# Cross-attention and a 16-expert layer on one core: outputs of the experts computed turned, with gates put on the hidden values, and first products eight experts ahead

## The reference, cut to what matters

```python
# x: (8, 56, 128); ctx: (8, 1500, 128); 16 heads of 64; HIDDEN 256; 14 routed + 2 shared experts
x = x + tanh(g_xattn) * attention(layernorm(x), ctx, ctx)      # causal by index: only keys 0..55 count
xf = layernorm(x).reshape(448, 128)
gates = softmax(xf @ router_w)                                 # (448, 14)
masked = top2(gates); masked = masked / (masked.sum(-1) + 1e-9)
def ffn(rw, W1, W2):
    h = xf * rsqrt(mean(xf * xf) + 1.1920929e-07) * rw
    return silu(h @ W1) @ W2
routed = einsum('end,ne->nd', [ffn(e) for e in routed_experts], masked)
x = x + tanh(g_ffn) * (routed + sum(ffn(s) for s in shared_experts))
```

## Time and profile before

| | |
|---|---|
| runs | 117.8, 117.86, 119.21 us |
| profiled execution | 117.94 us, its span 116.1 us (first to last instruction) |
| PE busy | 107.2 us, 92% |
| DVE, ACT, POOL busy | 69.3, 59.4, 43.8 us |
| clock granted to PE | full in every slice |
| DMA | 13.76 MB, all loads landed by 40.3 us |

### The profile page before, as it was taken

The page is one execution under the profiler, slowest core; times in us unless marked ns, Lnnn a source line. Parts: engine busy times, 40 slices in busy tenths (PEclk is TensorE's granted clock), DMA queues, the critical chain, the costliest instruction groups (busy, mean ns, idle before and its releaser), DMA issues.

```text
span 116.1 us, 2394 instructions
## 1 busy us (share of the span) xinstructions
PE 107.2 (92%) x826; PEld 91.6 (79%) x826; DVE 69.3 (60%) x195; ACT 59.4 (51%) x99; POOL 43.8 (38%) x75
## 2 busy tenths in 40 slices
PE   6699999996999999999699999999999999999980
PEld 6687768745496487488489989999999999999970
DVE  0068966659688789879843329999333333333360
ACT  5053787943579579579964298333333333333300
POOL 7803599000001000100101798666666666663000
PEclk9999999999999999999999999999999999999999
DMA  3899999999997000000000000000000000000003
GB/s 90 254 295 285 416 413 413 420 420 444 421 428 308 28 0 0 0 6 0 0 0 6 0 6 0 3 3 0 0 6 0 0 0 0 0 0 0 0 0 79
DMA packets 3169, 13.76 MB, mean 119 GB/s; under 512 B 431, under 2 KB 1007, under 8 KB 2775
## 3 DMA queue, kind: packets, MB, share of 16 engines
q1 hardware_dynamic: 3159, 13.63, 31.3%
HBM read 13.40 MB, written 0.23 MB: 117 GB/s over the span
## 4 chain that ended last, share of the span: by engine, by line
PE 57%; DVE 14%; DMA 12%; ACT 8%; SPq 4%; issue 3%; DVEq 0%; ACTq 0%
PE score_ps L736 15%; DMA ctx_all<-in_ctx_dram 12%; PE attn_ps L736 8%; PE ring L729 6%; PE ring L731 6%; PE ring L730 6%; PE ring L597 5%; ACT square_junk L816 4%; PE score_ps L552 4%; PE attn_ps L621 3%; DVE probs L1046 3%; DVE row_sum L1039 2%; DVE row_max L1025 2%; DVE probs L1032 2%; PE score_ps L546 2%
## 5 line engine op out<-in xcount | busy, mean ns | idle before, releaser
L938 ACT ACTIVATE mixT<-ring 128x896 f32<-128x896 f32 x16 | 14.6, 917 | 26.9 <-PE ring L731 26.9
L736 PE MATMUL score_ps<-w,mixT 128*112 (+1 forms) x160 | 19.1, 273 | 0.2 <-ACT mixT L938 0.2
L736 PEld LDWEIGHTS score_ps<-w,mixT 128*112 128x112 f32 x160 | 18.7, 177 | 0.8 <-issue 0.3
L437 POOL TENSOR_TENSOR h_scale<-h_base,minus_half 112x1 f32<-112x1 f32 x4 | 2.2, 547 | 41.7 <-DVE h_base L1069 41.7
L1210 DVE SCALAR_TENSOR_TENSOR xn_rows<-score_ps,gates,xn_rows 112x128 f32<-112x128 f32 x36 | 10.1, 343 | 11.5 <-PE score_ps L736 11.3
L621 PEld LDWEIGHTS attn_ps<-wkq_space,mixT 128*112 128x112 f32 x128 | 14.2, 177 | 2.4 <-issue 2.4
L621 PE MATMUL attn_ps<-wkq_space,mixT 128*112 128x128 f32 x128 | 15.0, 276 | 0.0
L402 POOL TENSOR_TENSOR w_full<-w,columns 128x256 f32 (+1 forms) x16 | 9.8, 612 | 11.5 <-PE ring L731 10.5
L729 PE MATMUL ring<-hT_hi,w_hi 128*128 128x448 f32 (+2 forms) x36 | 13.9, 386 | 0.1
L731 PE MATMUL ring<-hT_hi,w_lo 128*128 128x448 f32 (+2 forms) x36 | 12.6, 350 | 0.0
L730 PE MATMUL ring<-hT_lo,w_hi 128*128 128x448 f32 (+2 forms) x36 | 12.6, 349 | 0.0
(11 more groups left out here) (136 smaller groups left out, 186.7 us busy)
## 6 DMA issues: line engine op xcount, KB each, us to landing
ctx_all<-in_ctx_dram SPq DMA_DIRECT2D x4, 1500.0 KB, 18.8
w<-in_w_dram SPq DMA_DIRECT2D x2, 1792.0 KB, 27.3
wkq_space<-in_wkq_dram SPq DMA_DIRECT2D x2, 512.0 KB, 6.1
wvo<-in_wvo_dram SPq DMA_DIRECT2D x1, 1024.0 KB, 10.6
w<-in_w_shared_dram SPq DMA_DIRECT2D x2, 256.0 KB, 16.4
ctx_head<-in_ctx_head_dram SPq DMA_DIRECT2D x1, 480.0 KB, 8.9
ctx_headT<-in_ctx_headT_dram SPq DMA_DIRECT2D x1, 224.0 KB, 4.9
x_space<-in_x_rows_dram SPq DMA_DIRECT2D x1, 224.0 KB, 5.7
```

What stands on the lines that cost most here:

```text
L736: last = nc.tensor.matmul(dst, hidden[slot][:, c, t * ROWS:(t + 1) * ROWS], w2_chunk(c), start=(c == 0), stop=(c == 1))
L938: nc.scalar.activation(hidden[slot], ring[:, 2 * slot:2 * slot + 2, 0:TOKENS], ACT.Silu).then_inc(S["hidden_ready"], 1)
```

## The change

- **Outputs turned.** `w2` is now the weight operand and `hidden` moves, 448 columns at a time; all experts add into one PSUM bank, `out_sums`, with the model dimension on the partitions. Experts 0 to 3 (`WHOLE`) use two fp32 products (L885); experts 4 to 15 (`PARTED`) use six fp32r products (L897, L899, L903). The output is (128, 448), turned back on the host.
- **Gates on hidden.** DVE multiplies the 128x896 hidden values of each routed expert by a tile of gates (L1454); for parted experts ACT rounds (L1121) and DVE subtracts (L1463). The gates of experts 2, 3 and 4 are spread over the partitions by PE (L942); those of 5 to 15 are stored to DRAM and loaded again with a broadcast, in four loads (L453, L456). The shared experts' gate is multiplied into their second weights by POOL (L578). PE also turns `x1` (L930) and the gates (L936).
- **First products ahead.** Eight hidden slots in the space of `keyproj`. PE does the first products of experts 2 to 9 before or between outputs 0 to 3, and is then seven ahead; ACT's order of Silu and rounding follows it. The loops are written out.
- **POOL.** It splits the first weights of all 16 experts and the second weights of 12, mostly while attention runs. `w_hi` is now a cast of `w_full` and waits for it. The four `h_scale` stand between these pieces.
- **SP.** The context keeps two pieces (four batches) at a time; its third and fourth piece wait for squares of earlier batches. Weights go through staging space (`stage_pair`, `ctx_head`, `wvo`), in pieces of four experts, each behind a wait for what used the space before.

```diff
+WHOLE = [0, 1, 2, 3]
+PARTED = [e for e in range(EXPERTS) if e not in WHOLE]
+FULL_SLOTS = 8
+PART_SLOTS = 4
+GATE_GROUPS = [(3, 4), (4, 5), (5, 7), (7, ROUTED)]
...
+            context(0)
+            context(1)
+            sp.dma_start(w2_whole[:, 0:SHARED, :, :], A["w2_shared"]).then_inc(S["w2_shared_loaded"], 16)
...
+            sp.wait_ge(S["ctx_lo_ready"], 1)
+            first_four(0)
+            sp.wait_ge(S["w1_scaled_ready"], SHARED)
...
+            wait_filled(sp, "M3")
+            first_four(1)
+            first_four(2)
+            context(2)
+            sp.wait_ge(S["w1_scaled_ready"], 6)
+            second_four(0)
+            context(3)
...
+            def split_w1(experts):
...
+                    nc.gpsimd.tensor_tensor(w1_full[:, :], first_weights(e),
+                                            rms_cols[:, e:e + 1].to_broadcast([P, HIDDEN]), ALU.mult)\
+                        .then_inc(S["w1_full_ready"], 1)
+                    pool.wait_ge(S["w1_full_ready"], e + 1)
+                    nc.gpsimd.tensor_copy(w1_hi[:, e, :], w1_full[:, :])\
+                        .then_inc(S["w1_hi_ready"], 1)
...
+            def split_w2(experts):
+                for e in experts:
+                    n = PARTED.index(e)
+                    weights = second_weights(e).rearrange("p (c d) -> p c d", c=2)
+                    pool.wait_ge(w2_loaded[n // 4], 16)
+                    nc.gpsimd.tensor_copy(w2_hi[:, n, :, :], weights)\
...
+            split_w1(range(6))
...
+            nc.gpsimd.tensor_copy(spread[:, :, :], ones).then_inc(S["spread_ready"], 1)
+            split_w1(range(6, 12))
+            second_scale(0)
+            split_w1(range(12, EXPERTS))
+            second_scale(1)
+            split_w2(range(4, 8))
...
+            second_scale(2)
+            split_w2(range(8, 12))
+            second_scale(PAIRS - 1)
...
+            def next_hidden(e):
+                pe.wait_ge(S["hidden_ready"], e - 1)
+                hidden_products(e).then_inc(S["hidden_filled"], 1)
...
+            for e in range(6, 9):
+                next_hidden(e)
+            output_whole(2)
+            next_hidden(9)
+            for e in range(3, EXPERTS - 1):
+                if e in WHOLE:
+                    output_whole(e)
+                else:
+                    output_parted(e, out_sums).then_inc(S["expert_done"], 1)
+                if e + AHEAD - 1 < EXPERTS:
+                    next_hidden(e + AHEAD - 1)
...
+            for e in range(9, EXPERTS):
+                round_hidden(e - 4)
+                silu(e)
...
-            def add_expert(place, gate, before=moe):
-                for t in range(PAIRS):
-                    last = nc.vector.scalar_tensor_tensor(
...
+                dve.wait_ge(S["hidden_ready"], e + 1)
+                nc.vector.tensor_tensor(hidden(e), hidden(e), tile.unsqueeze(1)
+                                        .to_broadcast([P, 2, TOKENS]), ALU.mult)\
+                    .then_inc(S["hidden_gated"], 1)
...
+            for e in range(SHARED, EXPERTS):
+                gate_hidden(e)
+                if e - 1 in PARTED:
+                    subtract_hidden(e - 1)
+            subtract_hidden(EXPERTS - 1)
```

More of the change, by code:

```diff
@@ new lines, in output_parted @@
+            def output_parted(e, sums, cols=slice(0, TOKENS)):
+                n = PARTED.index(e)
+                hi, lo = (hidden_part(slots, e) for slots in (hi_slots, lo_slots))
+                pe.wait_ge(S["w2_split_ready"], n + 1)
+                pe.wait_ge(S["hidden_hi_ready"], n + 1)
+                alone = e == EXPERTS - 1
+                for c in range(2):
+                    nc.tensor.matmul(sums, w2_hi[:, n, c, :], hi[:, c, cols],
+                                     start=(alone and c == 0), stop=False)
+                    nc.tensor.matmul(sums, w2_lo[:, n, c, :], hi[:, c, cols],
+                                     start=False, stop=False)
+                pe.wait_ge(S["hidden_lo_ready"], n + 1)
+                for c in range(2):
+                    last = nc.tensor.matmul(sums, w2_hi[:, n, c, :], lo[:, c, cols],
+                                            start=False, stop=(e >= EXPERTS - 2 and c == 1))
+                return last
@@ new lines, in _, with spread_gates @@
+            last.then_inc(S["x1T_filled"], 1)
+            next_hidden(4)
+            pe.wait_ge(S["gates_ready"], 1)
+            for t in range(PAIRS):
+                last = nc.tensor.transpose(gatesT_ps[:, t * ROWS:(t + 1) * ROWS], gates[:, t, :],
+                                           ident[0:ROWS, 0:ROWS])
+            last.then_inc(S["gatesT_filled"], 1)
+            next_hidden(5)
+            def spread_gates(n):
+                nc.tensor.matmul(gate_banks[n], spread[:, n, :], gates_parts, start=True, stop=True)\
+                    .then_inc(S["gate_spread"], 1)
@@ L960, in _ @@
+            for e in range(5, 9):
+                silu(e)
+            round_hidden(4)
+            for e in range(9, EXPERTS):
+                round_hidden(e - 4)
+                silu(e)
+            for e in range(EXPERTS - 4, EXPERTS):
+                round_hidden(e)
         @block.vector
@@ L1205, in wide @@
                 return col[:, :].unsqueeze(2).to_broadcast([ROWS, PAIRS, ROUTED])
-            def add_expert(place, gate, before=moe):
-                for t in range(PAIRS):
-                    last = nc.vector.scalar_tensor_tensor(
-                        out=moe[:, t, :], in0=out_banks[place][0:ROWS, t * D:(t + 1) * D],
-                        scalar=gate(t), in1=before[:, t, :], op0=ALU.mult, op1=ALU.add)
-                last.then_inc(S["acc_done"], 1)
-            def static_gate(e):
-                return lambda t: gates[:, e, t:t + 1]
             dve.wait_ge(S["logits_filled"], 1)
```

392 lines of the change are left out of this document (235 added, 157 removed).

## The result

| | before | changed |
|---|---|---|
| median of the runs side by side | 117.83 us | 120.5 us (119.93 to 121.09) |
| profiled execution: time, span | 117.94, 116.1 us | 120.87, 119.0 us |
| `x1` of tile 3 taken up by DVE (end of attention) | 62.39 us | 70.16 us |
| from there to the end of DVE's last addition | 51.08 us | 46.76 us |
| from there to the end of the span | 2.63 us | 2.08 us |

The changed kernel takes 1.022 of the time before (95% interval 1.015 to 1.030; measured again with more runs: 1.0215, 1.0165 to 1.0264). It is slower, by 2.1 to 2.2%, and neither interval tells whether that is over 2%. Forecast was 118.3 us, 0.4% slower, range 114.0 to 122.2.

A forecast was written before the change was run, and what follows sets the result against it. Before: PE bounds the expert layer, hand-overs attention. After: attention ends at 69.4 us (7.0 late), expert 5 gated from 88.2, DVE done 113.0, closing 1.5, store 2.1: span 116.6, time 118.3 us, range 114.0 to 122.2.

The forecast's parts named there:

- POOL's chain: Attention: POOL's list runs without pause from 25.6 us, h_scale of tile 2 comes 7.4 us late, attention ends 7.0 late.
- The cast: POOL's cast of 256 elements, shown by no row: taken as 0.39 us, between ends of 0.26 and 0.61.
- Collisions: Attention: six two-input DVE normalisations meet a busy POOL and lose 0.15 us each, 0.9 us in all.
- The 1.2 us that this rule was said to add for the casts: Attention: if any GpSimd operation locks the shared ports, casts collide too and the sum is some 1.2 us higher.
- The gates' path: Start of expert layer: DVE's gate operations take 4.6 us, then 6.8 us until expert 5 can be gated, at 88.2.
- the way through DRAM shifts 23 DVE operations one for one: Rival on late gates, expert layer: each delay reaches the end; 2 us more gives 120.3 us; chance 0.07.
- DVE behind the gates: Expert layer from 88.2 us: 11 multiplications and 12 subtractions take 23.0 us, plus 1.7, last subtraction ends at 113.0.
- PE's 5.6 us are given away to POOL's lateness and to DVE: Summary: POOL's lateness (7.0 us) and DVE's two 1 us operations an expert behind the gates use up PE's gain.
- PE's gain itself: Expert layer: turned outputs save PE 7.2 us, transposes and spreading products add about 1.6, 5.6 gained if PE stayed bound.
- The end behind it: Kernel end, behind the closing addition at 114.5 us: a single store issue until the span ends, 2.1 us.
- The clock: Rival: PE idles near 48 and 61 us, half clock adds 3.8 us on the last attention output: 122.1; chance 0.10.
- the rival on collisions: Attention and gates: normalisations lose up to 0.6 us each, up to 3 us more, 119.5 to 121.5 us; chance 0.18.

The follow-up runs named there:

- e_scales_first: Changed kernel with POOL's list reordered, h_scale of tiles 0, 1, 2 behind 9, 13, 15 first weights, second weights behind the third scale: 114.06 us, ratio 0.963.
- b_late: Kernel before with 14, 4, 3 and 2 triples of scratch work on POOL ahead of the four scales, making them late: 127.63 us, ratio 1.076.
- e_warm: Changed kernel with 60 bf16 products on zeros, meant for PE's wait near 48 us: 121.98 us, ratio 1.029.
- b_busy: Kernel before with 8, 4, 4 and 3 triples of scratch work on POOL ahead of the four scales, none late: 118.74 us, ratio 1.008.
- b_casts: b_busy with the added POOL work made of one-input casts and copies alone (11, 6, 6, 4 triples): ratio 1.009.
- s_gates_late: e_scales_first with the gates stored to DRAM twice before they are loaded, about 1.7 to 2 us later: 115.08 us, ratio 0.974.
- e_dve_less: Changed kernel with DVE's subtractions of experts 8 to 15 over 56 of 448 tokens only, 6.3 us less DVE work: 119.7 us, ratio 1.014.
- s_pe_less: e_scales_first without the product of the second weights' low part in the twelve parted experts, 4.9 us less for PE: 113.0 us, ratio 0.960.
- s_early_product: e_scales_first with PE's first product of expert 6 ahead of the three spreading products instead of behind them: 113.81 us, ratio 0.966.
- e_warm_both: Changed kernel with e_warm's 60 products and 48 more meant for PE's wait near 63 us: 120.62 us, ratio 1.019.

## Why the prediction came out as it did

- **POOL's chain: right.** Forecast 25.6 us for the start, 48.1 and 63.9 us for the scales of tiles 0 and 2; measured 25.7, 49.47 and 64.65. The cast was priced at 0.39 us and takes 0.39 to 0.40. Attention ended at 70.16 instead of 69.4. That this lateness reaches the end one for one was right (e_scales_first; b_late for the attention alone). The split over the tiles was not: some 3 us of waiting were forecast at tiles 0 and 2 each, 4.26 and 1.37 came, since the slow PE between them used up a part of the second (with a full clock there e_warm waited 2.84 us).
- **Collisions: right in kind, too small in size.** The prediction took 0.9 us. Where a busy POOL is never late, that fits: b_busy shows 0.8 us at `x1`, 0.16 us a normalisation. But in the changed kernel the chain goes through POOL, and POOL's own operations lost at least 1.85 us there. Without them its list took 37.1 us (25.73 to 64.65, less 1.85) where 37.4 was forecast, so the misses partly cancel, and the 0.8 us by which attention missed are what is left. The prediction left open whether casts collide, and b_casts decides that they do. That is what the Trainium skill says, page "SBUF — State Buffer", section on the two separate sides: a DVE operation with two SBUF inputs and a GpSimd operation that reads SBUF lock each other out, whichever starts first, for the whole instruction. The trace agrees on who is stretched (the three pairs above). The 1.2 us that this rule was said to add for the casts match the 1.16 us that they lost.
- **The gates' path: right in size, wrong in weight.** Forecast 4.6 and 6.8 us; measured 4.6 (77.64 to 82.26) and 7.0. But "the way through DRAM shifts 23 DVE operations one for one" fails: with 2 us more the stretch does not change (s_gates_late).
- **DVE behind the gates: the step that failed.** "PE's 5.6 us are given away to POOL's lateness and to DVE": DVE took next to nothing (0.48 us, e_dve_less). Its chain was sized rightly: forecast from `x1` of tile 3 to the last addition 114.5 − 69.4 = 45.1 us, and where DVE does bound, in s_pe_less, it is 44.90. But the sum took this for the length of the layer without laying PE's chain beside it. By the prediction's own numbers that chain is 51.1 (from 62.35 to the end of the last addition, 113.47) less 5.6, which is 45.5 us: 0.4 us longer, and the longer one counts. The rest is a term of the wrong size, PE's gain itself: 4.32 us in the stretch, not 5.6. The rows of PE show what was left out: a wait of 0.65 us for DVE's low part of the gates near 84 us, of which s_early_product gets 0.41 back, and the last expert in two halves (114.74 to 116.49, 1.75 us, where expert 13 takes 1.24). The sum of 0.4 and 1.3 is the layer's 1.7 us (46.76 against 45.1). The end behind it, forecast 2.1 us, took 2.08.
- **The clock: present, and not on the path where it fell.** Its rival had the mechanism (half clock behind PE's idle time, from about 50.3 us) and chance 0.10, but its price was that of the last attention output, behind the second wait, and there the clock stayed full in this execution. Behind the first wait POOL's list was later than the slow PE; behind the second the clock costs time, as e_warm and b_late show.
- **Total.** 116.6 was forecast for the span, 119.0 came: 0.8 from attention, 1.6 from the layer and the end. The net, 2% slower rather than 0.4%, lies between the forecast and the rival on collisions; 1 us of it is that rival's cause, the larger part is not. The forecast range was 8.2 us wide, and that 120.5 falls into it speaks for the large term, the late POOL; it says nothing for the account of the layer.

## What to carry to other kernels

When work moves to an idle engine, look at what else is in that engine's queue: here a list of 39 us (25.7 to 64.65) held up three operations of 0.55 us, on two of which the critical chain waited, and reordering the same list is worth 6.8 us, more than twice what the change lost. When two engines come out nearly full, sum both chains to their end and take the later one; a queue almost without gaps is not yet the bound, and taking work from each in turn (1.86 of 4.9 us arrive from PE, 0.48 of 6.3 from DVE) says which it is. Check in the trace that an experiment did what it was made for: the products of e_warm ran 8 us ahead of the wait that they were to fill, and those of e_warm_both past its end. Compare such experiments over the stretch in question in the trace, which repeats to 0.02 us here while the whole times spread by 1 to 3 us.

## What was not expected of the hardware

- The granted clock fell to half (1.2 GHz of 2.4) after PE had been busy 0.64 of 3 us, and stayed there from about 50.3 to 57.1 us (worked out from the means 0.55, 0.50 and 0.81 of the windows), while PE was busy for all of 53 to 56 us. In e_warm, with a wait of 1.5 us instead of 4.7 at that place, it stayed full and fell at the next wait (0.61 at 65 to 68 us, after PE had been busy 1.08 of 3 us). The Trainium skill, page "TensorE: Matmul & The Clock Gate", section on HAM oscillation, describes such falls where PE waits for DMA between bursts, again and again. The traces agree on the fall behind a wait, but here PE waited for DVE, and the clock fell once or twice in an execution; in the trace before it did not.
- In a collision the operation that starts later is stretched, on either engine: POOL's cast of 0.39 us takes 0.79 to 0.82, its subtraction of 0.73 takes 1.16, DVE's normalisation of 0.625 up to 1.03 us. Even DVE's normalisation of a tile, one tile and two columns, takes 0.62 to 0.63 us where it starts just behind a POOL operation (49.51 behind POOL's 49.45), against 0.34.
